# Cross attention: residual steps spread over the second context round, four waits regrouped. Grouped attention: turns, value products and scores each put together

## The reference

```python
x = x + L0_xattn(layernorm(x), ctx, mask, position_bias, ...)   # 32 heads of 128, softmax, w_out
x = x + L0_ffn(layernorm(x), ...)                               # silu(gate) * up, 1376 wide
x = x + L1_xattn(layernorm(x), ctx, ctx, mask, ...)             # 32 query heads on 8 key heads
x = x + L1_ffn(layernorm(x), ...)                               # 512x512 and LoRA of rank 16 x 8

# inside L0_xattn, the normalised x is itself the residual:
score = softmax(where(m, q @ k.T + position_bias, -inf))
return hidden_states + (score @ v) @ w_out.T
# inside L1_xattn: rope on q and k, then
logits = 30 * tanh(q @ k.T * 0.0884 / 30); softmax; @ v; @ Wo
```

## Time and profile before

| | us |
|---|---|
| median of 3 runs | 1614.78 |
| lowest and highest | 1614.23, 1615.2 |
| the profiled execution | 1615.26 |
| its span, first to last instruction | 1613.5 |
| PE busy in it | 1598.8 |
| DVE, POOL, ACT busy | 999.5, 878.4, 748.1 |

### The profile page before, as it was taken

The page is one execution under the profiler, slowest core; times in us unless marked ns, Lnnn a source line. Parts: engine busy times, 40 slices in busy tenths (PEclk is TensorE's granted clock), DMA queues, the critical chain, the costliest instruction groups (busy, mean ns, idle before and its releaser), DMA issues.

```text
span 1613.5 us, 25021 instructions
## 1 busy us (share of the span) xinstructions
PE 1598.8 (99%) x8512; PEld 1365.9 (85%) x8512; DVE 999.5 (62%) x1528; ACT 748.1 (46%) x1922; POOL 878.4 (54%) x688
## 2 busy tenths in 40 slices
PE   9989999999999999999999999999999999999999
PEld 7878888888888888888888887888898898889887
DVE  7523333636666676676679677776656656665675
ACT  5331111225454544554553334656645546654653
POOL 6344444537466575565569775544536435443445
PEclk9999999999999999999999999999999999999999
DMA  9434444513333332333341211101100111010011
GB/s 345 172 125 157 153 151 153 180 40 130 108 120 106 107 123 94 107 123 94 114 150 47 59 41 50 60 33 33 53 34 27 47 40 33 27 47 20 21 53 53
DMA packets 52111, 146.44 MB, mean 91 GB/s; under 512 B 7264, under 2 KB 12000, under 8 KB 51520
## 3 DMA queue, kind: packets, MB, share of 16 engines
q1 hardware_dynamic: 52032, 145.41, 26.0%
HBM read 107.64 MB, written 37.75 MB: 90 GB/s over the span
## 4 chain that ended last, share of the span: by engine, by line
PE 94%; DVE 2%; POOL 1%; ACT 1%; issue 1%; DMA 0%; SPq 0%; ACTq 0%; DVEq 0%; POOLq 0%
PE banks L55 27%; PE banks L57 26%; PE banks L56 26%; PE banks L2283 4%; PE banks L783 3%; PE banks L803 3%; PE banks L792 2%; PE banks L2290 2%; PE banks L224 1%; ACT resid L993 0%; DMA rawA<-in_x_wK 0%; DVE resid L1933 0%; POOL wtA_lo L1428 0%; ACT x_probs L1055 0%; DMA g_swapped<-in_l_b 0%
## 5 line engine op out<-in xcount | busy, mean ns | idle before, releaser
L2747 POOL TENSOR_TENSOR g_swapped<-g_swapped,rawB 128x512 f32<-128x512 f32 x80 | 103.0, 1290 | 171.2 <-ACT g_swapped L2429 171.2
L1526 POOL TENSOR_TENSOR x_probs<-x_probs,x_inv 128x512 f32<-128x512 f32 x64 | 66.6, 1040 | 170.9 <-DVE x_inv L1317 168.0
L1055 ACT ACTIVATE x_probs<-x_probs,x_top 128x128 f32<-128x128 f32 x256 | 99.5, 390 | 92.2 <-DVE x_top L1308 92.2
L1428 POOL TENSOR_TENSOR wtA_lo<-rawA,wtA_hi 128x1024 fp32r<-128x1024 f32 (+1 forms) x31 | 72.1, 2326 | 100.2 <-ACT wtB_hi L964 78.8
L1193 DVE COPY c_v_kept<-banks 128x512 f32<-128x512 f32 x64 | 44.1, 690 | 108.1 <-PE banks L57 108.1
L2577 DVE TENSOR_TENSOR g_turned_by<-banks,rawB 128x512 f32<-128x512 f32 x80 | 55.2, 690 | 85.8 <-ACT g_swapped L2429 85.8
L2741 POOL TENSOR_TENSOR g_probs<-g_probs,g_inv 128x512 f32<-128x512 f32 x64 | 67.7, 1079 | 74.5 <-DVE g_inv L2568 74.4
L55 PE MATMUL banks<-wtV_hi,g_att_lo 128*128 128x512 f32 x256 | 104.3, 407 | 0.0
L55 PE MATMUL banks<-xT_hi,wtO_lo 128*128 128x512 f32 x256 | 102.9, 402 | 0.0
L2428 ACT COPY g_swapped<-banks 64x512 f32<-64x512 f32 x80 | 46.7, 583 | 120.3 <-PE banks L57 113.6
L56 PE MATMUL banks<-wtV_lo,g_att_hi 128*128 128x512 f32 x256 | 100.3, 392 | 0.0
(11 more groups left out here) (353 smaller groups left out, 5155.2 us busy)
## 6 DMA issues: line engine op xcount, KB each, us to landing
kept_k<-c_k_kept SPq DMA_DIRECT2D x16, 1024.0 KB, 4.0
x_k<-kept_k SPq DMA_DIRECT2D x32, 512.0 KB, 4.5
kept_v<-c_v_kept SPq DMA_DIRECT2D x14, 1024.0 KB, 4.9
x_v<-kept_v SPq DMA_DIRECT2D x28, 512.0 KB, 3.5
rawA<-in_x_wQ SPq DMA_DIRECT2D x16, 512.0 KB, 4.4
rawO<-in_x_wO SPq DMA_DIRECT2D x16, 512.0 KB, 3.5
rawO<-in_g_wQ SPq DMA_DIRECT2D x16, 512.0 KB, 3.5
rawV<-in_g_wO SPq DMA_DIRECT2D x16, 512.0 KB, 3.5
```

The lines of the kernel that those rows point to most:

```text
L1055: e = nc.scalar.activation(probs[:, b, :], probs[:, b, :], ACT.Exp, bias=top[:, b:b + 1], accum_out=total[:, b:b + 1])
L1428: return pool.tensor_tensor(wt[into][1][:, cut], raw[kind][:, cut], f32(wt[into][0][:, cut]), ALU.subtract)
L1526: pool.tensor_tensor(probs[:, part, :], probs[:, part, :], rows, ALU.mult).then_inc(probs_ready, 1)
L2747: pool.tensor_tensor(part, part, sin[:, :].unsqueeze(1).to_broadcast([P, HB, P]), ALU.mult)\
```

## The change

In the cross attention:
- ACT's eight `add_hidden` of round 1 stand one, three, three and one around `high(5)`, `high(6)` and `high(7)`, and no longer behind the round's last weights. POOL's `twice_of` moves from the end of round 1 to the end of round 0.
- The first three parts of `seven_keys(1, 0)` wait for the kept values 5, 6 and 7 one by one, where all waited for the eighth.
- DVE's `inverse(1, 1)` moves from the end of `first_pair` into `body(1)`, between the first query sum and the next ones, and ACT's `output_weights(0)` behind the attention copies and the first query copy of `body(1)`.
- The last outputs of batches 0 to 3 wait for the first half of `att_lo`, those of batches 4 to 7 for the second.

In the grouped attention, PE's order alone: all four turns behind Q1, value products 0 and 1 together ahead of Q3, 2 and 3 together behind it, scores 0 and 1 together behind the first output batch, scores 2 and 3 behind the third.

```diff
--- before.py
+++ after.py
@@ -677,13 +677,18 @@
                 n = key_step(i, which)
                 weights_ready("A", 2 + n + 1)
                 pe.wait_ge(qk_copied, 8 + 2 * n)
-                if isinstance(i, int) and i == 1 and which == 0:
-                    pe.wait_ge(vo_added, 8)
-                    key_twist.ready(pe, 4)
+                first = isinstance(i, int) and i == 1 and which == 0
+                if first:
+                    pe.wait_ge(vo_added, 5 + X)
                 else:
                     pe.wait_ge(q_sums, 5 * n)
                 part(X, a11, c11)
+                if first:
+                    key_twist.ready(pe, 4)
+                    pe.wait_ge(vo_added, 5 + Y)
                 part(Y, s2, ct2)
+                if first:
+                    pe.wait_ge(vo_added, 5 + Z)
                 part(Z, s1, ct1)
                 pe.wait_ge(qk_copied, 8 + 2 * n + 1)
                 part(X, a12, c21, True)
@@ -901,10 +906,11 @@
             first_head(2)
             pv(LAST, 1, 1)
             first_head(3)
-            pe.wait_ge(att_lo, 4 * PAIRS)
             for b in range(B):
                 if b >= HB:
                     first_head(b)
+                if b % HB == 0:
+                    pe.wait_ge(att_lo, 4 * PAIRS - 1 + b // HB)
                 output_part(LAST, b, 1, LAST_O).then_inc(vo_made, 1)
                 if b >= 4:
                     norm.turn(pe, b - 4)
@@ -1036,17 +1042,21 @@
                     high(4)
                 key_weights(key_step(i, 0) + 1)
                 if second:
-                    for b in range(5, B):
-                        high(b)
+                    add_hidden(0)
+                    high(5)
+                    for b in range(1, 4):
+                        add_hidden(b)
+                    high(6)
+                    for b in range(4, 7):
+                        add_hidden(b)
+                    high(7)
+                    add_hidden(7)
                 key_copy(i, 1)
                 key_quarter(i, 1)
                 if isinstance(i, int) and i == QUADS - 2:
                     last_key_weights()
                 else:
                     key_weights(key_step(i, 1) + 1)
-                if second:
-                    for b in range(B):
-                        add_hidden(b)
 
             def exps(n, j):
                 act.wait_ge(top_ready, 2 * n + j + 1)
@@ -1107,7 +1117,6 @@
                 probs_turned(0, 1)
                 exps(1, 0)
                 exps(1, 1)
-                output_weights(0)
 
             def body(g, last):
                 a, b_ = 2 * g, 2 * g - 1
@@ -1116,6 +1125,8 @@
                 attn_hi(a - 2, 0, 0)
                 first_copy(g)
                 attn_hi(a - 2, 1, 0)
+                if isinstance(g, int) and g == 1:
+                    output_weights(0)
                 first_quarter(g)
                 probs_turned(b_, 0)
                 probs_turned(b_, 1)
@@ -1332,12 +1343,14 @@
 
             s00, s01, s10, s11 = (q[:, h, token_half(j)] for h in range(2) for j in range(2))
 
-            def two_sums(g):
+            def first_sum(g):
                 dve.wait_ge(qk_copied, K_COPIED + 2 * g + 1)
                 if not isinstance(g, int) or g:
                     dve.wait_ge(scores_ready, 4 * g)
                 dve.wait_ge(qk_made, K_UNITS + 7 * g + 2)
                 query_sum(s01, Y, s10)
+
+            def next_sums(g):
                 dve.wait_ge(qk_made, K_UNITS + 7 * g + 5)
                 query_sum(s11, Y, s10)
                 dve.wait_ge(q_sums, K_SUMS + 5 * g + 2)
@@ -1358,7 +1371,8 @@
                 value(0)
                 value(1)
                 value(2)
-                two_sums(0)
+                first_sum(0)
+                next_sums(0)
                 value(3)
                 logits(0, 0)
                 fourth_sum(0)
@@ -1373,13 +1387,15 @@
                 logits(1, 0)
                 logits(1, 1)
                 inverse(1, 0)
-                inverse(1, 1)
 
             def body(g, last):
                 a, b_ = 2 * g, 2 * g - 1
                 attn_lo(a - 2, 0, 0)
                 attn_lo(a - 2, 1, 0)
-                two_sums(g)
+                first_sum(g)
+                if isinstance(g, int) and g == 1:
+                    inverse(1, 1)
+                next_sums(g)
                 logits(a, 0)
                 fourth_sum(g)
                 fifth_sum(g)
@@ -1468,6 +1484,7 @@
                     pool.wait_ge(power_set, 2)
                     scale_of(0)
                     scale_of(1)
+                    twice_of()
                     return
                 value_weights(i)
                 for which in range(2):
@@ -1479,7 +1496,6 @@
                         combine(n, n + 2, ("A", n + 2))
                         seven_low(n + 3)
                 if isinstance(i, int) and i == 1:
-                    twice_of()
                     mask_of()
                 if isinstance(i, int) and i == QUADS - 2:
                     value_weights(QUADS - 1)
@@ -2316,8 +2332,8 @@
                 weights_ready("Q", p)
                 query(r, u, 0)
                 query(r, u, 1)
-                turn(p - 1, 0)
-                turn(p - 1, 1)
+                for j in range(4):
+                    turn(p - 1, j)
                 query(r, u, 2)
                 second = r == 0 and u == 1
                 if second:
@@ -2325,22 +2341,20 @@
 
                 pe.wait_ge(proj_free, seq(r, 0, V_AT + 3) - (PER if u == 0 else 0) + 1)
                 pv(p - 1, 0, before_kv)
-                turn(p - 1, 2)
                 pv(p - 1, 1, before_kv)
-                turn(p - 1, 3)
                 if not second:
                     query(r, u, 3)
                 weights_ready("O", p - 1)
                 pv(p - 1, 2, before_kv)
+                pv(p - 1, 3, before_kv)
                 output_batch(r, u, 0)
                 scores(p, 0, rope_of(r, u, 1, 0))
-                pv(p - 1, 3, before_kv)
+                scores(p, 1, rope_of(r, u, 1, 0))
                 output_batch(r, u, 1)
-                for j in range(1, 4):
-                    scores(p, j, rope_of(r, u, 1, j // 2))
-                    if j < 3:
-                        output_batch(r, u, j + 1)
-                for b in range(4, B):
+                output_batch(r, u, 2)
+                scores(p, 2, rope_of(r, u, 1, 1))
+                scores(p, 3, rope_of(r, u, 1, 1))
+                for b in range(3, B):
                     output_batch(r, u, b)
                 if u == 0:
                     values(r)
```

## The result

The changed kernel takes 1621.7 us (median of six runs, 1620.68 to 1622.52) against 1614.59 us for the kernel before on the same chip: a ratio of 1.0044, with a 95% interval from 1.0031 to 1.0057. It is slower, by 0.4%, and 1.0 us over the forecast of 1620.7 us. The profiled execution's span is 1620.5 us, where that of before was 1613.5 us: +7.0 us.

What follows compares the result with a forecast made beforehand. TensorE (PE) was taken as the bound, busy 1598.8 of 1613.5 us. Cross attention -9.6 us and grouped attention +15.5 us gave +5.9 us, carried to the 1614.78 us median: 1620.7 us, 8-in-10 range 1616.5 to 1624.5 us.

Steps and rivals of the forecast that it cites:

- The 4.2 us stop: Cross attention, PE waiting behind ACT's key copy: removal gains 4.4 idle, 2.4 clock and 0.1 restart, 6.9 us.
- the eight activations fit into ACT's holes: Cross attention round one: three activations take 2.16 us, ACT idles 2.62 us before `high`, so nobody is delayed.
- The part for the clock: Cross attention: 12 products after the key-copy wait ran at the lower clock, 0.20 us lost each, 2.4 us regained.
- The three smaller waits: Eighth kept value 0.8 us, pair-one query sum 0.9 us, low part of last attention output 1.0 us: all gained.
- The price of moving Q2: Grouped bodies 2 to 15: Q2 0.88 us later makes value products 2 and 3 wait, 1.05 us each, 14.7 us.
- The chain: Grouped body behind Q2: ACT swap, POOL multiply, VectorE add, then low parts; every link moves 0.88 us later.
- PE's list would show 12 to 15 us of these waits: Profile sign: L2587, low parts of turned probabilities, should release PE some 30 times for 12 to 15 us.
- The term of -0.05 us for joining: Grouped body: putting turns and value products together saves 0.05 us per body, bounds 0 and 0.1 us.
- rival b: Grouped bodies: only one of two waits per body appears, 14 x 0.5 = 7 us, 1613.2 us; chance 6%.
- The first body: First grouped body, Q2 and Q3 both ahead of value products 0: costs 0.9 us, between 0.5 and 1.5 us.
- Rival (d): Grouped bodies: clock falls behind PE's stops, 2.4 us more per body, 34 us in all, 1655 us; chance 2%.
- The inverse behind POOL's sum: Pair one: 128x4 VectorE product, stretched to 2.12 us by POOL's sum, takes 0.16 us again, so 0.9 us gain stands.

Runs made afterwards that it cites:

- the turns alone: Kernel before with all four turns ahead of Q2, value products and scores in their old places: 1624.93 us, ratio 1.0061.
- one turn: Kernel before with only turn 2 moved ahead of Q2, the fourth turn staying in place: 1618.51 us, ratio 1.0028.
- products and scores only: Kernel before with value products 3 directly behind 2 and scores in pairs, turns in their old places: 1617.76 us, ratio 1.002.
- the output batch ahead: Changed kernel with the first output batch moved ahead of value products 2 and 3, which stay side by side: 1608.18 us, ratio 0.9958.
- the output batch between: Changed kernel with the first output batch put between value products 2 and 3: 1615.22 us, ratio 1.0.

## Why the prediction was right, and where a term was not

**Right as a whole:** slower, and 1621.7 us against 1620.7 us, inside the range. Its steps, by its own numbers:

**The 4.2 us stop (6.9 us).** The run with this edit alone gained 6.95 us, and the clock at 106 to 110 us is full. That the eight activations fit into ACT's holes is shown by the idle time that is left before each `high` (1.55, 0.49 and 0.50 us). The part for the clock is less sure than it looks: the run with the turns alone, which keeps the 4.2 us stop, had a low clock of 3.4 us behind it, where before had 6.8 us. By the distances between starts the whole place costs 7.1 us in before's trace and 6.1 us in that of the turns alone. It isn't the turns that make this difference, for the kernel before shows it by itself: of its 22 executions beside this run, 12 have a mean clock of 0.999 and took 1614.3 us on average, and 10 have 0.998, which is what 6.8 us at half the clock make, and took 1615.3 us. The run with this edit alone is 6.4 us under the first and 7.3 us under the second. So 6.9 us is right for the mixture, and that the forecast from one trace came out to 0.05 us is partly luck.

**The three smaller waits (2.7 us).** All three are gone from the list; none was tried by itself. Together they gave 1.8 us by the medians, and 2.1 to 2.3 us if both the run with the residual activations alone and that with the whole cross part are compared with the executions of before at 0.999 only, or at 0.998 only: somewhat less than forecast. The first scores of the grouped attention come at 1018.75 us on average over the eight traces with all the cross edits, and at 1028.2 us over the five that have none of them (before, and the grouped part, the turns, one turn, products and scores only), so the whole part is worth 9.5 us (single traces lie up to 1.2 us off their mean), and the forecast was 9.6 us.

**The price of moving Q2 (0.54 + 0.49 + 0.1 - 0.05, taken as 1.05 us).** Measured 14.83 / 14 = 1.06 us. The chain was as written, link for link, and the three runs that break it (low parts first, turns behind Q2, the output batch ahead) bring 12.3 to 14.2 of the 14.8 us back, each with a different edit: shown. The inner split was a little off. The wait before value products 2 is 0.63 us and not 0.54 us (their start comes 0.15 us behind the end of the low part, and not 0.06 us, which is what value products 3 and the last body show). Value products 3 follow 1.10 us behind them where six products take 0.71 us: 0.39 us and not 0.49 us. Their sum is 1.02 us, against 1.03 us forecast, since it depends only on when low turned 3 is ready. That PE's list would show 12 to 15 us of these waits was wrong: it shows 10.4 us, for it leaves out the tail of the product before each and the late product behind it.

**The term of -0.05 us for joining** holds. In the run with the turned parts first it looks as if it had the wrong sign, since its bodies are 0.05 us longer than before's, but they still hold a wait of 0.12 us with its late product. With such waits taken off by the distances between starts, the bodies of the changed kernel, of the run with the turned parts first and of that with turns 2 and 3 behind Q2 are 0.07 to 0.08 us shorter than before's, and those with products and scores joined or with the output batch ahead 0.04 us. Why joining gains this was not looked into.

**Both waits, or one (rival b).** Both came. The run with the turns alone has one, 0.69 us per body, and the one with products and scores alone has 0.20 us; together they make 0.89 us and not 1.06 us, because joined to late turns the second wait is longer. The price given for this rival, 1613.2 us, is 1613.0 us by its own terms.

**The first body (0.9 us): the mis-sized term.** The stop itself with the second wait is worth 0.9 us, as forecast; in the first trace the body cost 2.49 us, 1.6 us of it the low clock. The median came out only 1.0 us over the forecast also because the cross attention won 0.65 us more than forecast. Rival (d), a fall of the clock behind a stop, had 2 in 100 because the stop of 0.8 us behind L2587 has none. It is true for none of the 14 bodies, whose stops are 0.47 and 0.16 us in the lists, and true in part of the executions for the one stop of 1.37 us. I weighed the rival as all or nothing and priced it at 34 us; the likelier form, that it strikes at the one stop that the change makes longer, stood nowhere. I also drew on the Trainium skill (TensorE: Matmul & The Clock Gate, What's actually happening), where recent activity releases the throttle: the trace agrees for the stops of half a microsecond that I applied it to, the clock is full through all 14 bodies, and it gives no help on the 1.37 us, where both outcomes were measured.

**The inverse behind POOL's sum.** Away from POOL's sum the 128x4 product takes 0.16 us and POOL's scaling follows at once, so the 0.9 us was not eaten. By the rule cited from the Trainium skill (SBUF — State Buffer, Who interferes with whom, on the port pair shared by VectorE and GpSimd) it had to be 0.16 us, and the trace agrees. The 0.9 us were not measured apart from the other two small terms.

**A better kernel.** The cross part alone, 1606.3 us, is the fastest of all that ran, 0.56% under before; with the new order on PE and the turned parts first on ACT and VectorE it is 1606.76 us, no different by measurement.

## What to carry to other kernels

Before work that is ready is pulled ahead on the busiest engine, look at what it pushes back: here two turns of 0.44 us, moved by a few microseconds, delayed the start of the longest chain of other engines by some 0.85 us and cost 0.69 us a body, though PE had the same work to do. Two steps that wait for two links of one chain should have other work between them, or the chain should bring these two links first. And read the distances between starts beside the list of waits: a wait shorter than the tail of a matmul stands in no list, and 14 of them are 2 to 3 us.

## What the hardware showed that I had not expected

- One stop of 1.37 us in a PE that is busy all around it was followed by 3.4 us at the lower clock in two traces (the changed kernel, and the grouped part alone) and by the full clock in four (the changed kernel once more, the turns alone, turns 2 and 3 behind Q2, the output batch between), all with a stop of 1.37 or 1.38 us. Stops of 0.83 to 0.94 us at the same place had the full clock in the traces of the eight other kernels, before among them. The same kernel shows both, so the order of its work does not decide it. The executions without a trace say the same. Of the 27 with this stop in kernels that no longer have the 4.2 us stop, five have a mean clock of 0.999 (four of eleven of the changed kernel, one of six with turns 2 and 3 behind Q2, none of ten with the output batch between) and the rest 1.000; of the 23 with the shorter stop all have 1.000. Among the kernels that keep the 4.2 us stop, one execution of before (1617.99 us) and one of the one-turn run (1622.25 us) have 0.997, that is, more low clock than the 6.8 us of the traces; where it lies is not shown. Of the first products of a kernel the Trainium skill says (TensorE: Matmul & The Clock Gate, What's actually happening) that the number of slow ones differs between runs of the same kernel; the two traces of the changed kernel differ in that way too, though in the middle of it. What in a run decides was not tried.
- After a wait on DVE, PE's next product started 0.15 us behind the end of DVE's instruction in the first wait of each body and 0.05 us in the second one, 1.1 us later; with the output batch ahead, it was 0.26 us at low attention 0. I can't say why. The first product behind a stop also keeps the next one off for 0.19 to 0.22 us where the pace is 0.12 us.
- A 4.2 us stop was followed by a low clock of 6.8 us in four traces (before, the grouped part, one turn, products and scores) and of 3.4 us in one (the turns alone). By the mean clocks both happen in the same kernel, about equally often, and the time differs by 0.9 us. A price read from one trace of a stop behind which the clock falls is unsure by that much.
